# Rotary products of local attention: the sine part added by accumulating transfers from GpSimd instead of a swap and an addition

## The reference

```
q = l2norm(q) * qs ; k = l2norm(k) * ksc          # 16 heads of 64
q = q * cos * scale + rotate_half(q) * sin * scale
k = k * cos / scale + rotate_half(k) * sin / scale
out = local_attention(q, k, v)                     # windows of 32, each looks at itself and the one before
x = out @ Wo + x ; x = ffn_layer(shift_tokens(x)) + x
```

## Time and profile before

| | |
|---|---|
| median of 3 runs | 5023.8 us (5016.67 to 5025.26) |
| the profiled execution, its own time | 5043.72 us |
| span in its profile | 5041.9 us |
| busy, share of the span | TensorE 80%, VectorE 74%, ScalarE 62%, GpSimd 21% |
| granted TensorE clock, mean | 0.945 |

### The profile page before, as it was taken

How to read it: one execution, slowest core, us unless ns; L and a number is a source line. 1 busy time by engine, 2 the same in 40 slices (tenths; PEclk the granted TensorE clock), 3 DMA queues, 4 the chain that set the end, 5 groups by cost and what they waited for, 6 DMA issues and landing times. The chain is left out here.

```text
span 5041.9 us, 174816 instructions
## 1 busy us (share of the span) xinstructions
PE 4035.4 (80%) x68188; PEld 2875.6 (57%) x68188; DVE 3716.5 (74%) x6687; ACT 3142.5 (62%) x8425; POOL 1080.8 (21%) x856
## 2 busy tenths in 40 slices
PE   7948888888888888888888888888888888884358
PEld 4625665666666666666656665565666665652134
DVE  4837777777777777777777777777787787765655
ACT  4716666666776676776666666666666667661123
POOL 0002222222222222222222222222222222210011
PEclk9959999999999999999999999999999999996679
DMA  0012222222222222222222222222222222220000
GB/s 26 1 57 86 73 77 71 83 86 75 78 73 75 89 85 75 75 75 82 86 76 70 77 73 85 81 79 73 76 74 90 77 77 73 73 65 3 0 9 13
DMA packets 126159, 336.66 MB, mean 67 GB/s; under 512 B 32592, under 2 KB 33744, under 8 KB 125264
## 3 DMA queue, kind: packets, MB, share of 16 engines
q1 hardware_dynamic: 125520, 326.63, 20.1%
HBM read 22.41 MB, written 2.10 MB: 5 GB/s over the span
## 5 line engine op out<-in xcount | busy, mean ns | idle before, releaser
L1172 ACT ACTIVATE loc_probs<-loc_pair,loc_ebias,loc_rnorm 128x64 f32<-128x64 f32 x3072 | 1200.4, 432 | 11.6 <-DVE loc_ebias L1332 8.4
L873 POOL TENSOR_TENSOR loc_ks<-loc_mcos,loc_swapped 128x1024 f32<-128x1024 f32 x192 | 451.9, 2354 | 1771.7 <-DVE loc_kr L1320 1378.2
L920 PE MATMUL loc_pair<-loc_hs,loc_wqk 128*128 128x256 f32 x3072 | 750.8, 388 | 49.6 <-issue 45.3
L873 POOL TENSOR_TENSOR loc_qr<-loc_mcos,loc_swapped 128x1024 f32<-128x1024 f32 x192 | 452.1, 2355 | 1283.2 <-DMA loc_swapped<-loc_msin 1207.1
L1172 ACT ACTIVATION_READ_ACCUMULATOR loc_probs<-loc_pair,loc_ebias,loc_rnorm 128x1 f32 x3072 | 717.2, 233 | 0.0
L920 PEld LDWEIGHTS loc_pair<-loc_hs,loc_wqk 128*128 128x128 f32 x3072 | 568.3, 192 | 153.9 <-issue 66.3
L1330 DVE TENSOR_REDUCE loc_mx<-loc_pair 128x8 f32<-128x512 f32 x384 | 264.6, 689 | 413.7 <-PE loc_pair L964 399.0
L1272 DVE SCALAR_TENSOR_TENSOR loc_mcos<-loc_pair,loc_scal,loc_tab 128x1024 f32<-128x1024 f32 x384 | 490.5, 1277 | 85.1 <-ACT loc_sq L1154 66.7
L1154 ACT ACTIVATE loc_sq<-loc_pair 128x1024 f32<-128x1024 f32 x384 | 396.7, 1033 | 207.0 <-PE loc_pair L920 207.0
L1281 DVE SCALAR_TENSOR_TENSOR loc_msin<-loc_pair,loc_scal,loc_tab 128x1024 f32<-128x1024 f32 x384 | 489.7, 1275 | 9.1 <-DMA loc_swapped<-loc_msin 8.5
L964 PE MATMUL loc_pair<-loc_kr,loc_qr 64*32 64x64 f32 x24576 | 320.7, 225 | 126.7 <-issue 126.1
(11 more groups left out here) (240 smaller groups left out, 7440.5 us busy)
## 6 DMA issues: line engine op xcount, KB each, us to landing
loc_swapped<-loc_msin SPq DMA_DIRECT2D x768, 256.0 KB, 2.6
loc_veven<-loc_vodd SPq DMA_DIRECT2D x768, 64.0 KB
loc_veven<-loc_vodd SPq DMA_DIRECT2D x384, 128.0 KB
loc_wqk<-wqk_dram SPq DMA_DIRECT2D x12, 512.0 KB, 4.7
loc_wv<-wv_dram SPq DMA_DIRECT2D x6, 512.0 KB, 4.4
loc_wo<-wo_dram SPq DMA_DIRECT2D x6, 512.0 KB, 4.4
x<-xT_dram SPq DMA_DIRECT2D x1, 2048.0 KB, 7.3
loc_tab<-tables_dram SPq DMA_DIRECT2D x1, 2048.0 KB, 7.5
```

What stands on the lines that cost most here:

```text
L873: nc.gpsimd.tensor_tensor(dst, mcos[i % 2][:, :], swapped[:, :], ALU.add).then_inc(rope_add, 1)
L920: ins = nc.tensor.matmul(pairs[b][:, p // 2, (p % 2) * UNIT:(p % 2 + 1) * UNIT], wqk[:, k, w:w + P], hs[u.odd][:, :], start=True, stop=True)
L1172: ins = nc.scalar.activation(probs[x][:, p, hp, :], pairs[b][:, hp, p * 2 * WIN:(p + 1) * 2 * WIN], ACT.Exp, bias=ebias[x][:, k:k + 1], sc ...
```

## The change

GpSimd no longer adds. VectorE writes the cosine product straight into `ks` or `qr`, and the sine product into one of two `msin`. GpSimd then issues two transfers of 64 partitions by 1024 elements, which read `msin`, exchange even and odd partitions, and add onto the destination while they move (`accum_op=ALU.add`). `ks` gets a second buffer, `msin` too; `mcos` and `swapped` are gone. SyncE keeps the `even_windows` and the weights. What waited for `rope_add` now waits for `swap_ready[i]`: TensorE's `scores` for i = 2, 3, VectorE's `scale_keys` for i = 0, 1, and the sine product i for the landing of the one two places before it, which read the same `msin`.

```diff
-        mcos = [sb(f"mcos{i}", [P, HALF_Q]) for i in range(2)]
-        msin, swapped = sb("msin", [P, HALF_Q]), sb("swapped", [P, HALF_Q])
-        qr, ks = [sb(f"qr{i}", [P, PAIRS, UNIT]) for i in range(2)], sb("ks", [P, PAIRS, UNIT])
+        msin = [sb(f"msin{i}", [P, HALF_Q]) for i in range(2)]
+        qr, ks = ([sb(f"{s}{i}", [P, PAIRS, UNIT]) for i in range(2)] for s in ("qr", "ks"))
...
+        def rotated_part(i, u):
+            g = 4 * (i % 2)
+            return (ks if i < 2 else qr)[u.odd][:, g:g + 4, :]
+
+        def landed(eng, i, n):
+
+            if not isinstance(n, int) or n >= 0:
+                eng.wait_ge(swap_ready[i], SWAP * n + SWAP)
...
-                after(sp, rot, u.n, 8, 2 * i + 2)
-                own_wait(sp, passed)
-                after(sp, rope_add, u.n, 4, i)
-                own_wait(sp, passed)
-                for half in range(2):
-                    sp.dma_start(swapped[1 - half:P:2, :], msin[half:P:2, :]).then_inc(swap_ready[i], 16)
...
-                nc.gpsimd.tensor_tensor(dst, mcos[i % 2][:, :], swapped[:, :], ALU.add).then_inc(rope_add, 1)
+                after(pool, rot, u.n, 8, 2 * i + 2)
                 own_wait(pool, passed)
+                for half in range(2):
+                    there = rotated_part(i, u)[1 - half:P:2, :, :].rearrange("p g t -> p (g t)")
+                    pool.dma_start(there, msin[i % 2][half:P:2, :], accum_op=ALU.add).then_inc(swap_ready[i], 16)
...
-                after(pe, rope_add, u.n, 4, 4)
+                for i in (2, 3):
+                    landed(pe, i, u.n)
+                    own_wait(pe, passed)
...
-                after(dve, rope_add, u.n, 4, i - 1)
+                if i < 2:
+                    after(dve, kr_ready, u.n - 2, 2, 2)
+                else:
+                    after(dve, sim_ps, u.n - 2, 2, 2)
...
-                after(dve, swap_ready[i - 1], u.n - (i == 0), SWAP, SWAP)
+                landed(dve, i - 2, u.n - (i < 2))
...
-                after(dve, rope_add, u.n, 4, 2)
+                for i in range(2):
+                    landed(dve, i, u.n)
```

More of the change, by code:

```diff
@@ L693, in local_layers @@
         w1_ready, w2_ready = sem("w1_ready"), sem("w2_ready")
-        hs_ready, qk_ps, sq_ready, rot, rope_add = sem("hs_ready"), sem("qk_ps"), sem("sq_ready"), sem("rot"), sem("rope_add")
-        swap_ready = [sem(f"swap_ready{i}") for i in range(4)]
+        hs_ready, qk_ps, sq_ready, rot = sem("hs_ready"), sem("qk_ps"), sem("sq_ready"), sem("rot")
+        swap_ready = [ctx.enter_context(nc.semaphore(f"loc_swap_ready{i}")) for i in range(4)]
         norm_ps, nT_ready, nT_ps, norm_read, rnorm_ready = sem("norm_ps"), sem("nT_ready"), sem("nT_ps"), sem("norm_read"), sem("rnorm_ready")
@@ L781, in step @@
             def step(at, refill=lambda name: None):
-                halves_across(1, at(2))
                 refill("wk")
-                halves_across(2, at(2))
                 even_windows(0, at(3))
-                halves_across(3, at(2))
                 refill("wq")
-                halves_across(0, at(1))
                 even_windows(1, at(3))
@@ L860, in tokens, with halves_across @@
                 nc.gpsimd.tensor_copy(scal[u.odd][:, :], params[:, bass.ds(u.layer, 1), 0:2].rearrange("p l k -> p (l k)")).then_inc(hs_ready, 1)
-            def rotated(i, u):
+            def halves_across(i, u):
                 if u is None:
                     return
[L865 to L869, removed]
+                after(pool, rot, u.n, 8, 2 * i + 2)
                 own_wait(pool, passed)
-                g = i % 2
-                dst = (ks if i < 2 else qr[u.odd])[:, 4 * g:4 * g + 4, :].rearrange("p g t -> p (g t)")
-                nc.gpsimd.tensor_tensor(dst, mcos[i % 2][:, :], swapped[:, :], ALU.add).then_inc(rope_add, 1)
+                for half in range(2):
+                    there = rotated_part(i, u)[1 - half:P:2, :, :].rearrange("p g t -> p (g t)")
+                    pool.dma_start(there, msin[i % 2][half:P:2, :], accum_op=ALU.add).then_inc(swap_ready[i], 16)
             def key_tail(u):
@@ L892, in step @@
             def step(at):
-                rotated(0, at(2))
+                halves_across(0, at(2))
                 ffn_params(at(5))
-                rotated(1, at(2))
+                halves_across(1, at(2))
                 key_tail(at(2))
-                rotated(2, at(2))
+                halves_across(2, at(2))
                 tokens(at(1))
-                rotated(3, at(2))
+                halves_across(3, at(2))
             pipelined(pool, step)
@@ L1278, in rotate_sin @@
                     return
-                after(dve, swap_ready[i - 1], u.n - (i == 0), SWAP, SWAP)
+                landed(dve, i - 2, u.n - (i < 2))
                 k = 0 if i >= 2 else 1
-                nc.vector.scalar_tensor_tensor(msin[:, :].rearrange("p (g t) -> p g t", g=4), flat(b).rearrange("p (g t) -> p g t", g=4),
+                nc.vector.scalar_tensor_tensor(msin[i % 2][:, :].rearrange("p (g t) -> p g t", g=4), flat(b).rearrange("p (g t) -> p g t", g=4),
                                                scal[u.odd][:, k:k + 1], bcast_mid(tab[:, 2 * k + 1, bass.ds(u.place * UNIT, UNIT)], 4),
@@ L1319, in scale_keys @@
                 at = WIN + BLK * x
-                nc.vector.tensor_tensor(kr[u.odd][:, :, at:at + BLK], ks[:, :, BLK * x:BLK * x + BLK],
+                nc.vector.tensor_tensor(kr[u.odd][:, :, at:at + BLK], ks[u.odd][:, :, BLK * x:BLK * x + BLK],
                                         flat(b).rearrange("p (g t) -> p g t", g=PAIRS), ALU.mult).then_inc(kr_ready, 1)
```

5 lines of the change are left out of this document (1 added, 4 removed).

## The result

The changed kernel takes 5008.6 us (median of 20 runs, 4994.01 to 5020.29) against 5025.45 us for the kernel before (20 runs beside them, 5013.86 to 5045.4 and one of 7349.86 us, which the ratio leaves out): 0.9965 times, 95% interval 0.9954 to 0.9976. It is faster by 0.35%, 17 us, in place of the 242 us forecast. Its profiled execution took 5011.75 us, with a span of 5009.9 us and a mean granted clock of 0.930 (before: 0.945).

What follows compares the result with a forecast made beforehand. It saw no single saturated engine but a ring of engines, worth what TensorE stops waiting for: 2.52 us a step over 96 steps, 242 us, from 5023.8 to 4782 us (-4.8%), everything else zero; range 4680 to 5035.

Steps and rivals of the forecast that it cites:

- rival A: GpSimd holds VectorE's way into SBUF while issuing transfers, about as long as its additions did: 5024 us, no change; chance 0.12.
- VectorE's held operations: VectorE's bias and Newton operations stand still under GpSimd's additions: 550 us of busy time, 5.7 us a step, which go.
- The three waits of 2.68 us a step: TensorE's waits for the gated product (79.9 us), inverse root (38.1) and ScalarE's squares (37.2), taken whole as going.
- the sum: The three waits less 6% for GpSimd's remaining key-tail multiplication: 2.52 us a step, 96 x 2.52 = 242 us gained.
- which nothing in this change touches: TensorE's idle time of kind "issue", 75.6 and 52.5 us, 2.2 us a step, taken as unchanged.
- TensorE waits for two landings in place of one addition: Waits and buffers at TensorE: two landings replace one addition, with as many matmuls around it; counted as zero.
- Traffic as zero: Transfer engines busy 0.25 of the time, at half if accumulation doubled every byte's time; zero on the path, being covered.
- B: Rival: GpSimd's eight issues a step become the bound from 5.2 us each; at 5.5 us each 5245 us; chance 0.13.
- C: Rival: accumulating transfers land late or crowd ScalarE's values' transfers, a new wait of 1 to 2 us a step: 4926 us; chance 0.15.
- the bounds of 2.6 and 9.9: Time from product to landing: 2.6 us as SyncE's like transfers, 9.9 us with two 2.35 us issues and doubled transfer.
- the 14.45 that there are: Cover: us from the product to TensorE's scores, whose mask product starts at 2530.86; some 12 left if the step shrinks.
- The delay beside a VectorE copy: Skill's account cited partly for B: a GpSimd-issued transfer of 0.62 us took 3.1 us beside a VectorE copy.

Runs made afterwards that it cites:

- small additions: Kernel before the change, with GpSimd's addition covering 16 of 1024 columns and the destinations set to zero once at the start: 4792.98 us, 0.9533 times before.
- moved by 128: 128 semaphore increments run once ahead of TensorE's loop, moving its code: changed kernel 4780.14 us (0.9501 times before); kernel before 5046.28 us (1.0045).
- by 192: Changed kernel, complete, with 192 semaphore increments run once ahead of TensorE's loop, which move its code: 4911.13 us, 0.9764 times before.
- tiny transfers: Changed kernel, with each accumulating transfer moving 16 instead of 1024 elements per partition: 4964.45 us, 0.9862 times before.

## Why the prediction was right and wrong

**Direction and range.** Faster it is, and 5008.6 us lies in the range of 4680 to 5035. That is luck: the range reached so far up to take in rival A, which fell, and the forecast of 4782 is off by 227 us.

**VectorE's held operations: right.** Forecast 550 us; VectorE's busy time fell from 3716.5 to 3140.7 us, 576. Rival A, that an issue holds VectorE as an addition does, falls: the biases beside an issue took 170 ns at most, and the 92 copies of norms beside one 684 ns in the median, as the others did. The Trainium skill's rule cited for it ("SBUF — State Buffer", "Who interferes with whom") held here.

**The three waits of 2.68 us a step: two right, one wrong.** The gated product's and the inverse root's went from (79.9 + 38.1) / 58 = 2.03 us a step to about 0.1. The squares' 0.64 did not go (36.4 us still, and 38.3 with small additions): the held bias was not what made ScalarE late, and the chain from it over the centring, read from one place of the timeline, was no proof for all 33. In the kernels moved by 128 and by 192 this wait is not on the list, so it depends on when TensorE comes there. All waits for engines fell by 1.82 us a step, where the sum had 2.52.

**The size, where only the hold is removed: right.** 237 us of 242 by the kernel with small additions. The match is in part luck: the 0.60 us a step that the sum took for the squares did not come, and an effect that the sum did not have made up for it. With TensorE standing still less, its time at work was 0.58 us a step less, with 68 us of the loop at 1.2 GHz in place of 154.

**The step that failed** is the one on the waits that stay: "issue", "which nothing in this change touches", and "TensorE waits for two landings in place of one addition, with as many matmuls around it. Zero." The work around it was the same, the number of instructions was not, and the length and place of its code is a cost by itself. "Issue" grew from 3.16 to 4.65 us a step, and the slow clock behind the gap came on top: in the loop TensorE is at 1.2 GHz for 154 us before and for 314 us after. By the runs this is worth 4793 to 4964 us, 171 of the lost 216. That difference also holds the issues on GpSimd and the other buffers; that these cost little is seen from the changed kernel moved by 128, which has them all and takes 4780.

**Traffic as zero: wrong by 42 to 44 us at this place of the code.** The rest of the loss. The sum looked for it at the landing, where there is cover; it came through the fetching of instructions, which the prediction had not among the users of the transfer engines: 0.26 of the 0.42 us a step between the changed kernel and the one with tiny transfers is "issue", and the rest time at work. The packets are there in the page of both kernels, and from 1500 to 4000 us there are 343 before and 373 after, 12 and 13 for an iteration. With time 0 at the branch, the changed kernel starts three of them at -6.9, -2.6 and +1.6 us (medians) and goes on 2.0 us behind the landing of the third. The kernel before starts its own at -5.0, -1.1 and +2.4 us and goes on 2.0 us behind the second. With tiny transfers the third starts at +1.0. The Trainium skill's "Advanced Engine Details and Errata", section "ISA Cache", gives such a piece as 16 KB or 256 instructions, and TensorE's store as 128 KB. By that, an estimate, 2846 instructions are 11.1 pieces and more than the store holds, so every iteration would fetch all its code again. The trace agrees, with its 12 or 13 fetches, and so does that moves by 64 instructions, by these figures a quarter of a piece, matter.

**Rivals B and C: refuted.** An issue costs 1.0 us where B needed 5.2. From the query product to the landing of the second transfer of its pair it is 7.0 us in the median, between the bounds of 2.6 and 9.9 and under the 14.45 that there are; TensorE never waits for a landing at the scores. The delay beside a VectorE copy that the prediction names for B doesn't show in the issues: no issue took over 1.2 us, and the 92 beside a copy of norms took 0.85 us in the median. ScalarE's wait for the values' transfers fell from 124.8 to 68.4 us, where C had it grow. That accumulating transfers eat a part was right in C, but not where it looked for it.

**What stays open.** Why a fetched piece comes in time in one kernel and late in another with as many pieces, and therefore how to choose a place without trying; why one pair of transfers issued later costs 80 us; and whether 128 would still be best after any further edit.

## What to carry to other kernels

When an engine's loop fetches its code anew in each iteration, as the queue "instruction" shows, its "issue" waits are a cost of their own: count the instructions that a change adds to that loop and the fetches in an iteration, and look at its branch and at the work behind it in the trace. Judge such a change at more than one place of the code (a few dozen harmless instructions ahead of the loop, in both kernels) before you keep or drop it, for the place alone was worth up to 4.6% here and hid a gain of 5%. Small VectorE operations whose maximum equals the length of a GpSimd addition are standing still for it, and moving the addition onto transfers frees them.

## What the runs showed of the hardware

- TensorE's code comes by transfers of 16384 bytes, 12 or 13 in an iteration of 2846 to 2854 instructions here. A branch back took 1.2 to 4.4 us in the median, depending on the place and length of the code, and at best 80 to 88 ns.
- 89 to 99% of TensorE's "issue" waits over 0.3 us, by time, ended 1.25 to 1.65 us behind the landing of such a transfer, or 1.9 to 2.15 us, mostly where they stood at the branch.
- After 4.6 us without work, TensorE was granted 0.50 (1.2 GHz) for its next 5.5 us, and eight matmuls took 3.78 instead of 1.99 us.
- Five semaphore instructions more in an iteration of 82 to 87 us cost 1.5 to 2%, while the matmuls right behind them waited for none of it ("issue" 0 and 0.4 us in 2500).
- An accumulating transfer from SBUF to SBUF of 64 x 4 KB costs GpSimd 1.0 us to issue and lands after 4.4 to 4.8 us; the same exchange without accumulation, from SyncE, landed after 2.6. Its issue didn't hold VectorE: 47 biases of the maxima beside one took 170 ns at most.
